# First cross attention of a Perceiver block: keys loaded in three transfers, and another order of its first transfers, key blocks, projections and score groups

## What is computed

```python
q = heads(layernorm(x)); k = v = heads(ctx)        # 16 heads of 16; ctx is 4096 x 256, no projection
u = einsum('hbqd,hbkd->hbqk', q, k) * scale / sqrt(16)
logits = where(mask, -inf, tanh(u) * exp(log_C))   # 256 queries x 4096 keys, for each head
x = x + moveaxis(einsum('hbqk,hbkd->hbqd', softmax(logits), v)) @ W_out.T
...
k1 = heads(ctx @ Wk.T + bk); v1 = heads(ctx @ Wv.T + bv)   # for the second layer's cross attention
```

## Time and profile before

| | us |
|---|---|
| three executions | 700.96, 703.43, 706.05 (median 703.43) |
| the profiled execution | 700.59 |
| its span in the profile | 698.8 |

### The profile page before, as it was taken

The page is one execution under the profiler, slowest core; times in us unless marked ns, Lnnn a source line. Parts: engine busy times, 40 slices in busy tenths (PEclk is TensorE's granted clock), DMA queues, the critical chain, the costliest instruction groups (busy, mean ns, idle before and its releaser), DMA issues. The chain is left out here.

```text
span 698.8 us, 14299 instructions
## 1 busy us (share of the span) xinstructions
PE 618.0 (88%) x5014; PEld 374.2 (54%) x5014; DVE 407.2 (58%) x899; ACT 453.5 (65%) x543; POOL 69.1 (10%) x151
## 2 busy tenths in 40 slices
PE   6888887887887888796799999999999998898998
PEld 5554444444344444464345555555554575674886
DVE  6467354222313225876798989898884326645634
ACT  2988999999999993682057767676777215503111
POOL 3001110000010000101211121211110000000000
PEclk8899999999999999998889999999999999999999
DMA  5886786376444113200027633322220570000000
GB/s 132 234 254 206 237 237 211 102 232 173 132 131 127 58 46 118 52 1 3 1 74 248 182 93 81 84 77 86 75 86 10 168 239 1 2 0 1 0 1 15
DMA packets 52904, 73.57 MB, mean 105 GB/s; under 512 B 11044, under 2 KB 29796, under 8 KB 52860
## 3 DMA queue, kind: packets, MB, share of 16 engines
q1 hardware_dynamic: 52091, 72.25, 35.0%
q10 hardware_dynamic: 768, 0.73, 0.4%
HBM read 58.90 MB, written 12.85 MB: 103 GB/s over the span
## 5 line engine op out<-in xcount | busy, mean ns | idle before, releaser
L1704 DVE TENSOR_REDUCE sb_m_blk<-ps 128x1 f32<-128x512 f32 x256 | 159.5, 684 | 18.5 <-PE ps L1550 17.2
L1486 ACT ACTIVATE sb_probs<-ps 128x1024 f32<-128x1024 f32 x128 | 125.8, 1025 | 49.9 <-PE ps L1580 49.3
L656 ACT ACTIVATE sb_probs<-ps 128x1024 f32<-128x1024 f32 x128 | 124.0, 1023 | 10.4 <-PE ps L721 8.9
L661 ACT ACTIVATE sb_probs<-sb_probs,sb_neg_cap,sb_cap 128x4096 f32<-128x4096 f32 (+2 forms) x34 | 121.9, 3591 | 0.1
L740 PE MATMUL ps<-sb_probs,sb_v_st 128*32 128x256 f32 x1024 | 74.5, 388 | 37.2 <-ACT sb_probs L661 37.2
L721 PE MATMUL ps<-sb_q_st,sb_k_st 112*128 112x256 bf16 x512 | 79.3, 280 | 5.2 <-DMA sb_k_st<-k_parts_l 4.4
L1580 PE MATMUL ps<-sb_q_st,sb_k_st 115*128 115x256 bf16 x512 | 76.3, 272 | 1.4 <-ACT sb_probs L1486 1.4
L1550 PE MATMUL ps<-sb_k_st,sb_q_m 96*128 96x512 bf16 x224 | 76.5, 383 | 0.0
L721 PEld LDWEIGHTS ps<-sb_q_st,sb_k_st 112*128 112x128 bf16 x512 | 42.9, 99 | 58.3 <-issue 28.9
L1596 PE MATMUL ps<-sb_probs,sb_v_st 128*32 128x256 f32 x1024 | 67.4, 384 | 0.2 <-ACT sb_probs L1486 0.2
L740 PEld LDWEIGHTS ps<-sb_probs,sb_v_st 128*32 128x32 f32 x1024 | 23.7, 108 | 64.8 <-ACT sb_probs L661 45.5
(11 more groups left out here) (284 smaller groups left out, 846.6 us busy)
## 6 DMA issues: line engine op xcount, KB each, us to landing
sb_k_st<-k_parts_l SPq DMA_DIRECT2D x223, 64.0 KB, 2.0
sb_k_st<-k_parts_l SPq DMA_DIRECT2D x93, 128.0 KB, 3.2
k_parts_l<-sb_v_proj SPq DMA_DIRECT2D x24, 256.0 KB
k_parts_l<-sb_early SPq DMA_DIRECT2D x48, 128.0 KB
sb_v_proj<-ctxT_blocks SPq DMA_DIRECT2D x8, 512.0 KB, 7.0
sb_v_rows<-ctx_by_pair SPq DMA_DIRECT2D x7, 512.0 KB, 4.2
sb_early<-ctxT SPq DMA_DIRECT2D x6, 512.0 KB, 3.8
sb_k_st<-k_parts_l SPq DMA_DIRECT2D x64, 32.0 KB, 1.8
```

Source lines behind the costliest of these rows:

```text
L656: a.activation(probs[:, slot, 4 * g:4 * g + 4, :], scores_bank(g), ACT.Tanh).then_inc(s["tanh"], 1)
L661: a.activation(part, part, ACT.Exp, bias=k.neg_cap[:, 0:1], scale=k.cap[:, 0:1]).then_inc(s["exp"], 1)
L1486: sc.activation(probs[:, g], scores_bank(g), ACT.Exp).then_inc(s["exp"], 1)
L1704: v.tensor_reduce(k.m_blk[:, b, q, blk:blk + 1], k.ps[:, m_bank(m_turn_of(idx)), :], AX.X, ALU.max).then_inc(s["m_read"], 1)
```

## The change

- **Keys of a unit in three transfers.** For each of the two blocks one transfer fills partitions 0 to 95 at once: its source is the 32 rows, repeated three times by a leading dimension of size 3 and step 0, its target 96 partitions. The low rows are loaded as before. The unit's bytes are the same.
- **First transfers.** Of the high part's copies into slot 0 GpSimd issues one for each half, so SP and ScalarE issue two in place of three; the store of block 0's high part goes behind the copies. VectorE does the reciprocal square root ahead of the residue. Three pieces of `busy` get one matmul more each.
- **Key blocks.** Block 1 is requested before SP waits for block 0's stores; the key projection's weights and first context block before unit 3's keys; the store of block 1 ahead of the value weights and of block 2. Blocks 2 to 7 are loaded later, blocks 4 to 7 split one iteration later (in iterations 2 and 3), in other buffers. The keys of unit 17 are requested after those of unit 18, behind the store of block 7.
- **Projections.** The first one goes where five `busy` matmuls were, and step 2 of iteration 0 has one in place of two. VectorE splits the projected keys of iteration 0 ahead of block 2.
- **Score groups.** `qk` of the next unit's group 0 goes one place ahead, before the third `pv` part.

The core of the diff:

```diff
+BLOCK_SLOT = (0, 1, 2, 0, 1, 2, 1, 2)
@@ load_k0_unit
-    for r in range(PARTS):
-        sp.dma_start(dst[2 * DH * r:2 * DH * (r + 1)], rows[0:2 * DH]).then_inc(loaded, 16)
+    for b in range(2):
+        thrice = rows[0:2 * DH, b].unsqueeze(0).to_broadcast([PARTS, 2 * DH, KSPLIT])
+        sp.dma_start(dst[0:MAXROW, b], thrice).then_inc(loaded, 16)
     sp.dma_start(dst[MAXROW:STACK0], rows[2 * DH:3 * DH]).then_inc(loaded, 16)
@@ first_hi
-        for r in range(PARTS):
+        for r in range(2):
             first_slot(eng, fold, 2 * DH * r, 0)
@@ sync
             first_hi(sp, 1)
-            store_part(k, sp, 0, 0, parts)
...
-            for p in (1, 2):
+            for p in range(PARTS):
                 store_part(k, sp, 0, p, parts)
+            load_block(k, sp, 1, blk)
             sp.wait_ge(k.sem("k0_stored0"), blocks_stored(0))
             load_first(0, 1)
-            load_block(k, sp, 1, blk)
-            for j in range(2, 4):
-                load_first(0, j)
-            (wk1)
+            load_first(0, 2)
+            (wk1, b1_k, ctx_blk)
+            load_first(0, 3)
+            store_block(1)
             (wv1)
-            (b1_k)
             (b1_v)
-            (ctx_blk)
+            next_pair(1)
             load_block(k, sp, 2, blk)
-            store_block(1)
-            next_pair(1)
-            load_block(k, sp, 3, blk)
             sp.wait_ge(k.sem("k0_stored1"), blocks_stored(1))
...
             (ctx_two)
-            store_block(2)
-            load_block(k, sp, 4, blk)
+            load_block(k, sp, 3, blk)
             sp.wait_ge(s["scores"], 12)
             load_first(1, 2)
-            for j in range(2):
-                store_kd1(0, j)
-            sp.wait_ge(s["proj"], 4)
-            (ctx_blk)
+            store_kd1(0, 0)
+            sp.wait_ge(s["scores"], 16)
             load_first(1, 3)
+            store_kd1(0, 1)
+            store_block(2)
             store_block(3)
-            load_block(k, sp, 5, blk)
...
-            for n in (6, 7):
+            for n in (4, 5):
                 sp.wait_ge(k.sem(f"k0_stored{n % 2}"), blocks_stored(n))
-            body(3, True)
+            for j in range(4):
+                sp.wait_ge(s["scores"], 48 + 4 * (j + 1))
+                if j != 1:
+                    load_late(4, j)
+                if j == 0:
+                    next_pair(4)
+                    next_ctx(3, 12)
+                if j < 2:
+                    store_kd1(3, j)
+                if j == 1:
+                    store_block(6)
+                if j == 2:
+                    store_block(7)
+                    for n in (6, 7):
+                        sp.wait_ge(k.sem(f"k0_stored{n % 2}"), blocks_stored(n))
+                    load_late(4, 1)
@@ gpsimd
+            pool.wait_ge(s["first_hi"], 1)
+            for fold in range(2):
+                first_slot(pool, fold, 4 * DH, 0, first_by_pool)
@@ step
                 qk(it, j, 3, first)
-                pv(pit, pj, 2, pfirst)
                 if ahead:
                     qk(nit, nj, 0, nfirst)
+                pv(pit, pj, 2, pfirst)
...
-                elif j >= 2:
-                    project(0, 2 * (j - 2), True)
-                    project(0, 2 * (j - 2) + 1, True)
+                elif j == 2:
+                    project(0, 1, True)
+                else:
+                    project(0, 2, True)
+                    project(0, 3, True)
@@ first_steps
-                busy(5)
+                project(0, 0, True)
...
-            for split, n in (("first_hi", 2), ("first_res", 3), ("first_mid", 5)):
+            for split, n in (("first_hi", 3), ("first_res", 4), ("first_mid", 6)):
@@ vector
-            dve.wait_ge(s["first_hi"], 1)
-            v.tensor_tensor(blk[:, 0], blk[:, 0], parts[:, 0, 0], ALU.subtract).then_inc(s["first_res"], 1)
             rsqrt(k, link, QT)
+            dve.wait_ge(s["first_hi"], 1)
+            v.tensor_tensor(blk[:, 0], blk[:, 0], parts[:, 0, 0], ALU.subtract).then_inc(s["first_res"], 1)
...
-            split_block(2)
-            copy_acc(0, 0)
             split_k(0, 0, True)
+            copy_acc(0, 0)
             split_k(0, 1, True)
+            split_block(2)
...
-            body(1, (FIRST_LATE, FIRST_LATE + 1))
-            body(2, (FIRST_LATE + 2, FIRST_LATE + 3))
-            with dve.Fori(3, H // 2) as it:
+            body(1)
+            body(2, {0: 4, 2: 5})
+            body(3, {0: 6, 1: 7})
+            for n in (6, 7):
+                dve.wait_ge(k.sem(f"k0_stored{n % 2}"), blocks_stored(n))
+            with dve.Fori(4, H // 2) as it:
```

More of the change, by code:

```diff
@@ L392, in blocks_loaded @@
 def blocks_loaded(n):
-    return 16 * (n // 3 + 1)
+    return 16 * BLOCK_SLOT[:n + 1].count(BLOCK_SLOT[n])
 def first_unit(k, h, half):
@@ L455, in turned, with first_slot @@
         return k.ps[0:STACK0, 6 + n % 2, :].bitcast(BF16)
-    def first_slot(eng, fold, row, part):
+    def first_slot(eng, fold, row, part, landed=None):
         eng.dma_start(k.k_st[row:row + DH, 0, fold * KSPLIT:(fold + 1) * KSPLIT],
-                      parts[2 * DH * fold:2 * DH * fold + DH, 0, part]).then_inc(first_in[fold], 16)
+                      parts[2 * DH * fold:2 * DH * fold + DH, 0, part]).then_inc(landed or first_in[fold], 16)
     def first_hi(eng, fold):
-        for r in range(PARTS):
+        for r in range(2):
             first_slot(eng, fold, 2 * DH * r, 0)
@@ L467, in first_mid @@
             first_slot(eng, fold, 2 * DH * r + DH, 1)
[L469 removed]
+    FIRST_LOADS = 2 * PARTS
     UNITS = 2 * H
@@ L493, in store_kd1, with next_ctx @@
                                  k.kd_bf[:, j, p, :]).then_inc(kd_out[j], 16)
-            def next_ctx(it):
-                sp.wait_ge(s["proj"], 4 * it + 4)
+            def next_ctx(it, projected=None):
+                sp.wait_ge(s["proj"], 4 * it + 4 if projected is None else projected)
                 sp.dma_start(k.ctx_blk[:, :, :], ctx_blocks[:, :, bass.ds(sp.snap(it * CBLK + CBLK), CBLK)]
@@ L564, in _ @@
                 if j == 0:
+                    sp.wait_ge(s["proj"], 4)
+                    sp.dma_start(k.ctx_blk[:, :, :], ctx_blocks[:, :, 2 * CBLK:3 * CBLK]).then_inc(s["blk_in"], 16)
                     next_pair(2)
@@ L711, in qk @@
                         pe.wait_ge(first_in[g // 2], 16 * FIRST_LOADS)
+                        pe.wait_ge(first_by_pool, 32)
                 elif g == 0:
-                    pe.wait_ge(k_in[j], 16 * K_LOADS * (it if j == 0 else it + 1))
+                    pe.wait_ge(k_in[j], 16 * K0_LOADS * (it if j == 0 else it + 1))
                     if j % 2 == 0 and not first:
@@ L763, in project @@
                     if first:
-                        pe.wait_ge(k.sem("w1_in"), 64)
+                        pe.wait_ge(k.sem("x_wk_in"), 48)
                         pe.wait_ge(s["q_stack"], H // 4)
+                if first and j == 2:
+                    pe.wait_ge(k.sem("w1_in"), 32)
                 if j >= 2:
@@ L893, in split_k, with v_rows @@
                 v.tensor_tensor(k.kd_bf[:, j, 2, :], k.kd_r[:, j, :], k.kd_bf[:, j, 1, :], ALU.subtract).then_inc(s["kd_split"], 1)
-            def v_rows(it, j, over_parts=False):
+            def v_rows(it, j):
                 dve.wait_ge(s["proj"], 4 * it + j + 1)
-                if over_parts:
-                    for n in (6, 7):
-                        dve.wait_ge(k.sem(f"k0_stored{n % 2}"), blocks_stored(n))
                 v.tensor_tensor(k.v_proj[:, bass.ds(4 * it + 2 * (j - 2), 2), :],
@@ L902, in v_rows, with body @@
                                 k.b1_v[:, :].unsqueeze(1).to_broadcast([P, 2, D]), ALU.add).then_inc(s["v_copied"], 1)
-            def body(it, blocks=None):
+            def body(it, blocks={}):
                 for j in range(4):
@@ L914, in body @@
                     else:
-                        v_rows(it, j, blocks is None and j == 2)
-                    if blocks is not None and j % 2 == 0:
-                        split_block(blocks[j // 2])
+                        v_rows(it, j)
+                    if j in blocks:
+                        split_block(blocks[j])
             def copy_acc(h, b):
@@ L934, in split_block @@
             def split_block(n):
-                x, out = blk[:, n % 3], parts[:, n % 2]
-                dve.wait_ge(k.sem(f"ctxT_in{n % 3}"), blocks_loaded(n))
+                x, out = blk[:, BLOCK_SLOT[n]], parts[:, n % 2]
+                dve.wait_ge(k.sem(f"ctxT_in{BLOCK_SLOT[n]}"), blocks_loaded(n))
                 if n >= 2:
@@ L953, in turned_to_stack @@
                               turned(n)[:, (h0 - 4 * n) * S:4 * S]).then_inc(s["q_stack"], 1)
-            dve.wait_ge(k.sem("x_in"), 16)
+            dve.wait_ge(k.sem("x_wk_in"), 16)
             norm_moments(k, link, k.x)
+            rsqrt(k, link, QT)
             dve.wait_ge(s["first_hi"], 1)
             v.tensor_tensor(blk[:, 0], blk[:, 0], parts[:, 0, 0], ALU.subtract).then_inc(s["first_res"], 1)
```

(1 more changed line is left out.)

29 lines of the change are left out of this document (16 added, 13 removed).

## The result

| | before | after |
|---|---|---|
| median (runs) | 703.16 us (6) | 777.73 us (6), 772.88 to 780.15 |
| profiled execution | 700.59 us | 775.19 us |
| its span | 698.8 us | 773.5 us |
| end of the first cross attention | 264.8 us | 337.9 us |

The ratio is 1.1046, with a 95% interval from 1.1007 to 1.1085: slower by 10.5%, some 20 us beyond the forecast's 758 and inside its range of 725 to 800.

The account below looks back on a forecast made before the run. ScalarE bounded the first cross attention before; after the change three DMA engines would. Stage +52.2 us plus 4.5 of holes gave 700.59 + 56.7 = 757.3 us, median put at 758, range 725 to 800 with 0.8 of the chance.

Parts of the forecast that it names:

- Three engines, the same three: Key transfers: the smaller outermost count, 3, decides, so they run on the same three of sixteen engines; chance 0.72.
- Rivals 2 and 3: Key transfers: target decides, sixteen engines, 697 us, chance 0.12; or three engines, others each time, 701 us, chance 0.04.
- 23.5 GB/s for one engine: Key transfers: speed of one DMA engine, taken from block 0's stores, with 24.1 and 19.2 as the ends.
- Rival 1: Key transfers: slower engines, 19.2 GB/s for all keys, +96.7 us, so 797 us; chance 0.12.
- The sum over the busiest engines: First cross attention: work of the three busiest DMA engines, 289.6 us, stage end 317.0 against 264.8, +52.2 us.
- holes: Behind the stores of blocks 3, 5 and 7, where SP waits for landing: 3 x 1.5 = 4.5 us on top.
- the path at the end: End of the stage: from the last keys at 304.6, 0.65 us to the tanh and 11.7 to the end.
- Single gaps: ScalarE waiting for keys: about 4 us at unit 1, 5 to 10 at units 4 and 8, 15 to 20 at unit 17.
- The forecast's signs: DMA slices near 2 or 3 tenths, under 100 GB/s; ScalarE idle some 55 to 60 us; last exp near 320.
- The first tanh: Start of the stage: GpSimd's copies cost 0, the earlier rsqrt 0 or 0.2 us either way at the first scores.
- the one on GpSimd's copies: Start: GpSimd's two copies land by 13.1 us, before the first scores at 15.79; cost 0 and no gain.
- The score group ahead: Group 0 0.56 us earlier, so eleven gaps of 0.15 go: -1.7 us while ScalarE bounds, 0 where keys do.

Follow-up runs that it names:

- run 11: The changed kernel with the key source repeated twice, the third copy by a transfer of its own: 791.0 us, ratio 1.1275 to the kernel before.
- run 1: The changed kernel with the old four key transfers of a unit, all else as changed: 701.49 us, ratio 0.9984 to the kernel before.
- Runs 7 and 9: run 1 with three-part key transfers for units 20 to 31 alone: 721.73 us; then also the context block requested ahead of the fourth unit's keys: 708.11 us.
- run 6: run 5 with block 0's first store ahead of the middle copies again and block 1 requested behind unit 1's keys: 698.57 us, ratio 0.9939.
- run 5: run 1 with loads, splits and stores of blocks 5 to 7 earlier and unit 17's keys requested one step sooner: 694.7 us, ratio 0.9868.

## Why the prediction was right, and where it was off

- **Three engines, the same three.** Shown: a share of 0.19 while only keys move, 0.13 with a repeat of two (run 11), and no spreading over time. The Trainium skill (DMA: Bandwidth & Descriptors, Rules for kernel authors) has this rule for a leading zero-step dimension; the trace of after agrees with it at 3, run 11 at 2. Rivals 2 and 3 (697 and 701) fall: with two units' keys in flight at 25 us the share is still 0.19.
- **23.5 GB/s for one engine.** Measured 23.4 in after, and 49/(0.13 x 16) = 23.6 in run 11 (24.5 if the share is 2/16). Rival 1 (19.2) falls, although its 797 is about as far from the result as 758: the 20 us that were missing came from elsewhere.
- **All of the loss in the key transfers.** Shown by run 1: 76 us with them, -1.2 without.
- **Its size.** The sum over the busiest engines gave +52.2 for the stage, which measured +73.1: 20.9 us are missing, for which the forecast had 4.5, and two of its steps failed. It takes three engines that are never idle, lets the last keys land at 304.6, and the stage end 12.4 us behind them. In after the stage's last load is a context block, and TensorE starts on it at 313.98:

```profile
301.91 1.68 SPq L420 DMA_DIRECT2D sb_k_st<-k_parts_l  x2
...
313.98 1.98 PE L802 MATMUL ps<-sb_early 128*128 128x512 f32 x4 [2.45 <-DMA sb_early<-ctxT]
...
315.00:320.00 5.00, 5.00 (x54) 2.71 (x53) 2.62 (x4) 3.71 (x5) 0.00 (x0) 1.00 0.02 3
```

The first step is the term called holes, 4.5 us in the forecast (1.5 at each of three places). The last load landed 9.4 us later than 304.6, and in windows of half a microsecond from 15 to 313 us the DMA share is under 0.1 for some 13 us, behind landings that SP waits for and in plain iterations where it waits for a free slot. The work itself was sized well: 299 us from 15 to 313.98 less 13 are 286, against the sum's 289.6. The second step is the path at the end. The last keys had landed by then, but the stage took 23.9 us more (313.98 to 337.93) in place of 12.4, because ScalarE was no longer waiting for keys: it had lost its time to context blocks and value pairs that stood behind keys. That is 9.4 + 11.5 of the 20.9. Runs 7 and 9 show this second loss by itself: a transfer with a short lead behind transfers with a long one costs some 13 us, over three iterations and at equal bytes.
- **Single gaps.** Unit 1 has 9.9 us (forecast 4): the unit ahead was done 2.5 us sooner than in before, SP requested the keys 2.07 later (21.38 against 19.31; forecast was 1), and from request to scores they took 9.8 us in place of 5.05, which is near the 4.2 more that the bytes give. Unit 8 has 12.8 behind a value pair (forecast 5 to 10), unit 17 has 17.7 (forecast 15 to 20, sized well), and unit 21 has 11.4 behind a context block, where no gap of that cause was forecast.
- **Luck in the number.** The sum gives 757.3 for the profiled execution; with the 2.8 us between it and the median that is 760, not 758. And the range holds the result only because its upper end is rival 1's 797, a slower engine that was not there; nothing in the sum stood for transfers that wait behind keys.
- **The forecast's signs.** ScalarE's idle time was to be 55 to 60 and is 85.6. The end near 320 was 337.9. Many of the first 15 slices of the page's DMA line were to stand near 2 or 3 tenths and under 100 GB/s. In after they read

```profile
DMA  5453445454543233123000384323222074000000
GB/s 136 125 184 124 144 139 154 149 163 142 166 142 124 88 115 114 62 77 76 1 3 1 104 242 143 86 77 88 83 77 86 4 231 136 2 1 0 1 1 14
```

That is mostly 4 and 5, and 115 GB/s or more in all but one, because the wide transfers still use all engines in between. A slice of 19 us is too long to show three busy engines; the windows of 2 to 10 us do.
- **The first tanh** was to stay within 0.2 us and comes 2.16 sooner. The step that failed is the one on GpSimd's copies: not their own landing was to be looked at, but what leaves SP's queue. SP's copies end at 13.12 (7.64 + 5.48) in place of 13.84 (10.43 + 3.41), because the store is out from among them, and run 6 shows that putting it back costs 1.65. TensorE's clock adds to it: at the first scores before it was granted 0.5 (1.2 GHz) and they took 1.86 us for eight; in after one window reads

```profile
13.00:14.00 1.00, 0.93 (x10) 0.74 (x8) 1.00 (x2) 0.60 (x1) 1.00 (x2) 1.00 0.32 70
```

The clock column has 1.00, that is 2.4 GHz. In run 6 it is 1.00 there too, with the first tanh at 16.10, so of the 2.16 us the greater part is the store's place; how the rest divides between the clock and GpSimd's two copies was not separated, nor was it shown that the added `busy` matmuls are what raised the clock.
- **The score group ahead** was to give 1.7 (eleven gaps of 0.15) and gives 6.0 alone, 4.4 within the change. The term was mis-sized because it was taken from marked gaps alone: the rows of before that carry none hold up to 0.17 us of waiting each.
- **The later splits** were costed at nothing beside the narrow keys. With wide keys they still cost 6.5 us at unit 17 (run 1), and run 5 gets 6.8 back.
- **The clock** fell to 0.5 after the long gaps, as forecast (the windows from 190 to 203.5 us).

What stays open: how much of the backlog in after belongs to each chain, since one gap resets the next; and the 4.45 us at unit 1 in the best version, where the three stores must land first and neither of two orders on SP helped the total.

## What to carry to other kernels

Count engines, not only bytes, before merging small DMA transfers: in this kernel a source repeated three times ran on three of sixteen engines at 23.4 GB/s each, and three transfers in place of four cost 76 us of 700. The sum of bytes over the busiest engines gave 52 of the 73 us; the rest came from requests that wait for a landing and from transfers with a short lead that queue behind those with a long one, so request the short ones first. And where a row joins several instructions, compare its length with the same row at its shortest before calling an engine busy: a reorder that looked like 1.7 us was worth some 5 to 6.

## What the runs showed of the hardware

- The narrow transfers delay the wide ones: 512 KB context blocks over sixteen engines landed 9.3 us after their request (median) where they had taken 3.8, although a share of 0.20 while one of them was under way (240 to 244 us) says that thirteen engines had next to nothing to do.
- One request for a source with a repeat took SP some 0.8 us (1.64 for the two below, L420), against 0.43 for a transfer of 32 rows in before (the earlier trace rows has three in 1.26), so the issue of three (21.38 to 23.51, 2.1 us) was longer than that of four (some 1.7). With transfers queued the same two took up to 4.66:

```profile
21.38 1.64 SPq L420 DMA_DIRECT2D sb_k_st<-k_parts_l  x2
23.06 0.45 SPq L421 DMA_DIRECT2D sb_k_st<-k_parts_l  x1
...
28.97 4.66 SPq L420 DMA_DIRECT2D sb_k_st<-k_parts_l  x2
```
